# An attention block whose query and key norms move from the operands to the scores, inside the instruction that takes the row maximum

## The reference

```python
def rms_norm(x, w):
    var = jnp.mean(x * x, axis=-1, keepdims=True)
    return w * x * jax.lax.rsqrt(var + 1e-6)
def attn(h):                                  # h: 2 x 512 x 512, 32 heads of 128
    q, k, v = h @ Wq + bq, h @ Wk + bk, h @ Wv + bv
    q, k = rms_norm(q, gq), rms_norm(k, gk)   # over all 4096 columns
    a = softmax(einsum('bhqd,bhkd->bhqk', q, k) / sqrt(128))
    return einsum('bhqk,bhkd->bhqd', a, v) @ Wo + bo
x = x + layernorm(attn(layernorm(x)))
x = x + layernorm(ffn(layernorm(x)))          # a base matrix and 8 gated low-rank experts
```

## Time and profile before

| What | Value |
|---|---|
| Time, median of 3 runs | 1174.58 us (1172.68 to 1175.04) |
| Time of the profiled execution | 1176.83 us |
| Its span, first to last instruction | 1175.0 us |
| TensorE busy | 1130.2 us (96%) |
| VectorE busy | 848.8 us (72%) |
| GpSimd busy | 724.2 us (62%) |
| ScalarE busy | 663.2 us (56%) |
| Mean granted TensorE clock | 0.989 of full speed |
| Chain that ended last: TensorE / VectorE | 91% / 4% |

### The profile page before, as it was taken

The page is one execution under the profiler, slowest core; times in us unless marked ns, Lnnn a source line. Parts: engine busy times, 40 slices in busy tenths (PEclk is TensorE's granted clock), DMA queues, the critical chain, the costliest instruction groups (busy, mean ns, idle before and its releaser), DMA issues.

```text
span 1175.0 us, 17897 instructions
## 1 busy us (share of the span) xinstructions
PE 1130.2 (96%) x5704; PEld 955.7 (81%) x5704; DVE 848.8 (72%) x1304; ACT 663.2 (56%) x1331; POOL 724.2 (62%) x360
## 2 busy tenths in 40 slices
PE   6999999999999699999999999999999999999796
PEld 5788888888888588888888888888888888888575
DVE  6445545545454688888888888888888888888886
ACT  4333333333333667767767767767767767776432
POOL 2543443444437867777777777777777777774522
PEclk9999999999999899999999999999999999999899
DMA  5634434334344477887776776876776776876501
GB/s 181 216 117 151 145 123 161 134 134 161 116 152 161 125 156 162 184 154 164 184 162 153 185 161 152 184 164 152 183 163 152 183 164 152 181 149 141 143 1 71
DMA packets 302972, 178.55 MB, mean 152 GB/s; under 512 B 269536, under 2 KB 269664, under 8 KB 298720
## 3 DMA queue, kind: packets, MB, share of 16 engines
q1 hardware_dynamic: 302944, 178.19, 59.8%
HBM read 75.40 MB, written 35.65 MB: 95 GB/s over the span
## 4 chain that ended last, share of the span: by engine, by line
PE 91%; DVE 4%; DMA 2%; ACT 1%; issue 1%; SPq 1%; POOL 0%; DVEq 0%; ACTq 0%
PE ps L834 30%; PE ps L832 30%; PE ps L833 30%; DMA wa_stage<-w_qk 1%; ACT ps L678 1%; DVE neg_max L1265 1%; DVE stats L1113 1%; DVE ptl L1286 1%; DVE qk_lo L1286 0%; DMA y<-x 0%; DMA pair_k<-pair_q 0%; PE ps L842 0%; PE ps L890 0%; SPq L276 0%; DVE rms_row L1221 0%
## 5 line engine op out<-in xcount | busy, mean ns | idle before, releaser
L402 POOL TENSOR_TENSOR acc<-acc,squares 128x1024 f32<-128x1024 f32 x60 | 144.8, 2414 | 192.1 <-ACT squares L590 192.1
L448 POOL TENSOR_TENSOR qk_lo<-qk_in,qk_hi 128x1024 fp32r<-128x1024 f32 x64 | 178.5, 2790 | 125.1 <-ACT qk_hi L647 125.1
L1184 DVE TENSOR_SCALAR qk_out<-ps,tab 128x512 f32<-128x512 f32 x128 | 103.2, 808 | 165.8 <-ACT squares L590 165.7
L590 ACT ACTIVATE squares<-ps,q_k_bias 128x512 f32<-128x512 f32 x128 | 87.7, 687 | 230.1 <-PE ps L834 230.0
L678 ACT ACTIVATE ps<-ps,neg_max 128x512 f32<-128x512 f32 x256 | 168.8, 659 | 74.5 <-DVE neg_max L1265 74.5
L1265 DVE TENSOR_REDUCE neg_max<-ps 128x1 f32<-128x512 f32 x256 | 169.5, 686 | 49.6 <-PE ps L834 49.6
L834 PE MATMUL ps<-xh,wa_lo 128*128 128x512 f32 x512 | 204.5, 399 | 0.0
L832 PE MATMUL ps<-xh,wa_hi 128*128 128x512 f32 x512 | 201.6, 394 | 2.5 <-DVE xl L1168 1.5
L833 PE MATMUL ps<-xl,wa_hi 128*128 128x512 f32 x512 | 202.0, 394 | 0.0
L1279 DVE SCALAR_TENSOR_TENSOR pair_q<-ps,row_inv,pair_q 128x512 f16<-128x512 f32 x256 | 174.4, 743 | 8.4 <-ACT pair_q L687 4.5
L833 PE MATMUL ps<-wv_lo,xh 128*128 128x256 f32 (+1 forms) x544 | 157.1, 289 | 0.0
(11 more groups left out here) (132 smaller groups left out, 2400.2 us busy)
## 6 DMA issues: line engine op xcount, KB each, us to landing
q_k_scratch<-qk_out SPq DMA_DIRECT2D x32, 1024.0 KB, 4.7
qk_in<-q_k_scratch SPq DMA_DIRECT2D x64, 512.0 KB, 4.6
wa_stage<-w_qk SPq DMA_DIRECT2D x32, 512.0 KB, 5.6
wv_stage<-w_v SPq DMA_DIRECT2D x16, 512.0 KB, 5.1
wo_stage<-w_o SPq DMA_DIRECT2D x16, 512.0 KB, 5.1
y<-x SPq DMA_DIRECT2D x8, 256.0 KB, 6.0
y<-bo SPq DMA_DIRECT2D x8, 256.0 KB, 4.1
pair_k<-pair_q SPq DMA_TRANSPOSE x128, 4.6
```

What stands on the lines that cost most here:

```text
L402: pool.tensor_tensor(acc[:, w, :], acc[:, w, :], squares[:, par, w, :], ALU.add).then_inc(acc_ready, 1)
L448: pool.tensor_tensor(qk_lo[:, s % 2], qk_in[:, s], f32(qk_hi[:, s % 2]), ALU.subtract).then_inc(qk_lo_ready, 1)
L1184: dve.tensor_scalar(qk_out[:, par, w, b * S:(b + 1) * S], ps[:, 4 * par + g, :], tab[:, w, bass.ds(h, 1)], tab[:, 2 + w, bass.ds(h, 1)], A ...
```

## The change

Queries and keys are used unscaled. `scale_qk`, `rms_row` and the spreading of the queries' factors go. The queries' factors stay one number per partition (`q_factor`, times 1/sqrt(128)), and only the keys' are spread (`k_row`). `maximum` becomes a `tensor_tensor_reduce`: scores x `k_row` x `q_factor`, written back to the same bank, with the row maximum in `row_max`; after every second block VectorE waits for it and a small `tensor_scalar` makes the negative. The high half of queries and keys moves from ScalarE to GpSimd (`split_qk`), and `low_pt` moves from VectorE to GpSimd, behind `high_pt` (at the very end of stage B two casts stay on VectorE). The order of items 0 to 3 is new: item 0's scores come right after the last projection, more of the value products are placed between the first items, and batch 1's factors come later. The stage for `w_base` is now `z`, so that load waits for nothing.

```diff
@@ sync
-            sp.wait_ge(qk_scaled, 4 * PAIRS)
             sp.dma_start(wb_stage, w_base).then_inc(ffn_loaded, 16)
@@ gpsimd
+            def split_qk(p, s, m):
                 pool.wait_ge(qk_loaded[s], 16 * p + 16)
-                pool.tensor_tensor(qk_in[:, s], qk_in[:, s], rms_row[:, :, b * S:(b + 1) * S],
-                                   ALU.mult).then_inc(qk_scaled, 1)
+                if not (isinstance(m, int) and m < 2):
+                    pool.wait_ge(scores_ready, 4 * m - 4)
+                pool.sem_inc(qk_begun, 1)
+                pool.tensor_copy(qk_hi[:, s % 2], qk_in[:, s]).then_inc(qk_hi_ready, 1)
                 pool.wait_ge(qk_hi_ready, m + 1)
                 pool.tensor_tensor(qk_lo[:, s % 2], qk_in[:, s], f32(qk_hi[:, s % 2]),
                                    ALU.subtract).then_inc(qk_lo_ready, 1)
...
-            pool.wait_ge(rms_row_ready, 2)
-            scale_qk(0, 0)
+            split_qk(0, 1, 1)
...
+            def low_pt(n):
+                pool.wait_ge(low_turned, 16 * n + 16)
+                pool.sem_inc(ptl_begun, 1)
+                pool.tensor_copy(ptl[...], pair_k[:, 1]...).then_inc(ptl_ready, 1)
...
-                if prepare:
-                    scale_qk(p + s // 2, (s + 2) % 4)
-                if turned:
-                    high_pt(n - 1, None)
+                high_pt(n - 1, None)
+                low_pt(n - 1)
                 if prepare:
-                    low_qk((s + 2) % 4, n + 2)
+                    split_qk(p + s // 2, (s + 2) % 4, n + 2)
@@ scalar
-                if prepare:
-                    prepare_qk((s + 2) % 4, n + 2)
...
                 if first:
-                    spread(1, (YB, YB + 1))
+                    evacuate_v(1, 0, VB)
+                    evacuate_v(2, 2, OB)
@@ tensor
             pe.wait_ge(qk_lo_ready, 1)
+            pe.wait_ge(qk_out_ready, done + 6)
             scores(0, 0, first=True)
+            pe.wait_ge(wv_lo_ready, 2)
+            pe.wait_ge(qk_out_ready, done + 8)
+            v_item(0, 0, VB)
+            pe.wait_ge(acc_ready, 2 * HEADS + 8)
+            pe.wait_ge(var_ready, 5)
+            column_sums(1, YB)
+            v_item(0, 2, OB)
             pe.wait_ge(qk_lo_ready, 2)
             scores(1, 1)
+            pe.wait_ge(vl_ready, 1)
+            v_item(0, 4, VB)
+            pe.wait_ge(var_ready, 6)
+            v_item(0, 6, YB)
+            pe.wait_ge(rms_row_ready, 1)
+            spread(1, YB + 1)
+            pe.wait_ge(vl_ready, 2)
             attend(0, 0, 0)
@@ vector
-                dve.tensor_reduce(neg_max[:, sl, i:i + 1], ps[:, SCORE + i, :], AX.X, ALU.max,
-                                  negate=True).then_inc(max_ready, 1)
+                dve.sem_inc(max_begun, 1)
+                dve.tensor_tensor_reduce(ps[:, SCORE + i, :], ps[:, SCORE + i, :], key_factors(b),
+                                         q_factor[:, TB * b + i:TB * b + i + 1], -3.0e38, ALU.mult, ALU.max,
+                                         row_max[:, sl, i:i + 1]).then_inc(row_max_ready, 1)
+                if i % 2:
+                    dve.wait_ge(row_max_ready, 4 * n + i + 1)
+                    dve.tensor_scalar(neg_max[:, sl, i - 1:i + 1], row_max[:, sl, i - 1:i + 1], -1.0, None,
+                                      ALU.mult).then_inc(max_ready, 2)
...
                 inverses(n, sl)
-                if turned:
-                    low_pt(n - 1)
                 for i in range(TB):
-                    low_halves(n, sl, i, first)
+                    low_halves(n, sl, i)
```

More of the change, by code:

```diff
@@ L642, in evacuate_v, with spread @@
                                ACT.Copy, scale=V_DOWN).then_inc(vh_ready, 1)
[L644 to L656, removed]
-            square(*BY_BATCH[7], 8 * PAIRS)
[L658 to L664, removed]
+            def spread(b, bank):
+                act.wait_ge(rms_spread, b + 1)
+                act.activation(key_factors(b), ps[:, bank, :], ACT.Copy).then_inc(rms_row_ready, 1)
+            spread(0, YB + 1)
+            square(*BY_BATCH[7], 8 * PAIRS)
             act.wait_ge(stored[0], 16 * PAIRS)
@@ L692, in v_bias_column, with step @@
                 act.wait_ge(bias_ready, HEADS + n + 1)
-            def step(p, s, weights, first=False, output=True, value=True, prepare=True):
+            def step(p, s, weights, first=False, output=True, value=True):
                 n = 4 * p + s
@@ L739, in pair_of_heads, with second_head, first_weights @@
                 step(p, 3, wo_part(p + 1, 1 - par, 0, 8 * p))
-            step(0, 0, first_wo, first=True, output=False, value=False)
-            step(0, 1, nothing, output=False)
-            step(0, 2, nothing)
+            def second_head():
+                evacuate_v(4, 6, YB)
+                spread(1, YB + 1)
+            def first_weights():
+                act.wait_ge(wv_loaded, 32)
+                split_wv(1, 1, 0)
+                split_wv(1, 1, 2)
+                first_wo()
+            step(0, 0, first_weights, first=True, output=False, value=False)
+            step(0, 1, second_head, output=False)
+            step(0, 2, nothing, value=False)
             step(0, 3, wo_part(1, 1, 0, None))
@@ L754, in _ @@
             step(PAIRS - 1, 1, nothing)
-            step(PAIRS - 1, 2, nothing, prepare=False)
+            step(PAIRS - 1, 2, nothing)
             def ffn_weights():
@@ L807, in _ @@
             LAST = 4 * PAIRS - 1
-            step(PAIRS - 1, 3, nothing, value=False, prepare=False)
+            step(PAIRS - 1, 3, nothing, value=False)
             ffn_weights()
@@ L892, in column_sums, with spread @@
                 ins.then_inc(col_sums, 1)
-            def spread(b, banks):
-                for w in range(2):
-                    pe.wait_ge(diag_ready, 2 * b + w + 1)
-                    pe.matmul(ps[:, banks[w], :], ones[:, :], factors(b, w),
-                              start=True, stop=True).then_inc(rms_spread, 1)
+            def spread(b, bank):
+                pe.wait_ge(diag_ready, b + 1)
+                pe.matmul(ps[:, bank, :], ones[:, :], key_factors(b), start=True, stop=True).then_inc(rms_spread, 1)
             done = 8 * (PAIRS - 1)
@@ L986, in _ @@
             scores(2, 0)
-            values(0, 2, 0, 2)
+            pe.wait_ge(vl_ready, 4)
+            pe.wait_ge(rms_row_ready, 2)
             pe.wait_ge(otl_ready, 1)
@@ L1242, in split_v @@
                                          op1=ALU.subtract).then_inc(vl_ready, 1)
-            split_v(1, 0, 1)
-            mean_squares(1, 2)
-            diagonals(1)
-            split_v(2, 2, OB)
-            dve.wait_ge(y_set, 16 * NT)
             def add_y(count, tile, bank):
@@ L1292, in add_rows, with step @@
                     add_y(2 * n - 5 + k, 2 * ((s + 1) % 4) + k, YB + k).then_inc(y_added, 1)
-            def step(p, s, first=False, turned=True, output=True, value=True, rows=True):
+            def step(p, s, output=True, value=True, rows=True):
                 n = 4 * p + s
@@ L1310, in step @@
                     add_rows(p, s, n)
-            step(0, 0, first=True, turned=False, output=False, value=False, rows=False)
-            step(0, 1, output=False, rows=False)
-            step(0, 2, rows=False)
+            for i in range(TB):
+                maximum(0, 0, 0, i, i == 0)
+            mean_squares(1, YB)
+            inverses(0, 0)
+            for i in range(TB):
+                low_halves(0, 0, i, True)
+            split_v(1, 0, VB)
+            diagonals(1)
+            split_v(2, 2, OB)
+            step(0, 1, output=False, rows=False)
+            split_v(4, 6, YB)
+            dve.wait_ge(y_set, 16 * NT)
+            dve.wait_ge(rms_row_ready, 2)
+            dve.wait_ge(q_factor_ready, 2)
+            step(0, 2, value=False, rows=False)
             step(0, 3)
@@ L1410, in _ @@
             for i in range(TB):
-                maximum(N + 1, 1, i)
+                maximum(N + 1, 1, 1, i)
                 if i == 1:
```

79 lines of the change are left out of this document (35 added, 44 removed).

## The result

The kernel is slower: 1218.47 us (median of 4 runs, 1214.28 to 1221.62) against 1174.22 us, a ratio of 1.0374 with a 95% interval of 1.0342 to 1.0407. The prediction was 1186.6 us, with a range of 1166 to 1208. The direction was right and the size was not: +44 us instead of +12, and the time lies outside the range.

A forecast was written before the change was run, and what follows sets the result against it. TensorE bounds the kernel before, at 11.03 us an item; VectorE's chain would after, at 11.35. The terms -8.4 + 58 x 0.32 + 0.67 + 1.2 = +12.0 us on the median 1174.58 give 1186.6 us, range 1166 to 1208.

The forecast's parts named there:

- Is anything else late?: Check of stage B's other engines: GpSimd's load 8.4 to 9.9 us, below 11, and its casts hidden with 1.3 us left.
- VectorE becomes the bound through its own chain: Steady items: VectorE's serial chain takes 11.35 us, 0.32 us more than TensorE's 11.03; chance 0.50.
- the part from the reciprocal to the first low half: One term of VectorE's chain in a steady item: 1.22 us, against 1.61 before.
- The reduce instruction: New maximum on VectorE: pace 0.75 us, maximum arriving 0.86 us after its start, accumulator read included; first pair 1.74 us.
- Rival (1): Steady items: the reduce costs what a low half costs, VectorE stays under TensorE, 1167.4 us; chance 0.24.
- rival (3): Steady items: the reduce is dear, 0.93 us, period 11.85 us, 1216 us; chance 0.13 including periods between 11.6 and that.
- The first items: Start of stage B: the new order brings item 4's first maximum from 437.49 to 429.1 us, 8.4 us gained.
- The replay: Step-by-step timing of the first items: item 0's scores at 379 us, first maxima of later items at 408.1, 417.7 and 429.1.
- The sign that the prediction had named for a wrong start: In the changed profile, item 4's first maximum later than 433 us would show the forecast wrong.
- The casts are hidden: GpSimd's low cast ends 17.2 us after the item's first maximum, before TensorE's `attend` starts at 18.5 us.
- the second sign of being wrong: In the changed profile, TensorE waiting for `ptl` from GpSimd would show the forecast wrong.
- TensorE keeps its clock: Steady items: TensorE's waits of 0.3 us are too short to risk the lower clock; it may fall once among first items.

The follow-up runs named there:

- experiment 9: The changed kernel with the paired negations made by a negating tensor_reduce and `row_inv` made by ScalarE: 1194.86 us, ratio 1.0181.
- experiment 2: The changed kernel with each negation of two maxima made by a negating tensor_reduce instead of tensor_scalar: 1211.43 us, ratio 1.0332.
- experiment 8: The changed kernel with negations by tensor_reduce, `row_inv` on ScalarE and `evacuate_o` moved behind the second negation: 1175.79 us, ratio 1.0026.
- experiment 4: The changed kernel with the negations moved to ScalarE, one small copy ahead of each exponential: 1194.45 us, ratio 1.0175.
- experiment 1: The changed kernel with the old reduce in place of the new one and its negation, norm's factors left out of the scores: 1187.93 us, ratio 1.0132.
- experiment 5: The changed kernel with the old reduce, the norm's factors left out of the scores, and `row_inv` on ScalarE: 1165.81 us, ratio 0.9926.

## Why the prediction was wrong

**The step that failed** is in "Is anything else late?": "GpSimd's own load is ... 8.4 to 9.9 us, below 11", and with it the casts "hidden". It weighed GpSimd's time against the period and the casts against `attend`, and never asked which instruction of VectorE lies beside them. The load itself was right (147.28 us of 200 is 8.5 us in 11.5). But while a cast, copy or subtraction of GpSimd is under way, VectorE's small `tensor_scalar` instructions stand still: in the kernel after the negation up to 1.84 us and `row_inv` up to 1.67. The sum had no term for this. Both are links of VectorE's serial chain, and the change added one of them and filled GpSimd around the other. The price is the difference between the kernel after and experiment 9, which differ in nothing but those small instructions: 1218.8 - 1194.2 = 24.6 us of span (23.6 by the medians), made up of 4.3 at the start, 16.3 in the 58 periods, 2.7 in the last step and 1.3 in the tail.

It could have been read from the trace of before. VectorE, then GpSimd, in one of the first items and after stage B:

```profile
407.09 1.00 DVE L1272 TENSOR_SCALAR row_inv<-row_rec 128x4 f32<-128x4 f32 x1
408.01 3.44 DVE L1286 CAST ptl<-pair_k 128x2048 fp32r<-128x2048 f16 x1
...
406.17 1.90 POOL L505 CAST pth<-pair_k 128x2048 fp32r<-128x2048 f16 x1
408.02 2.35 POOL L448 TENSOR_TENSOR qk_lo<-qk_in,qk_hi 128x1024 fp32r<-128x1024 f32 x1
...
1100.82 5.21 DVE L1286 CAST qk_lo<-pair_k 128x2048 fp32r<-128x2048 f16 x1 [1.42 <-DMA pair_k<-pair_q]
...
1100.44 4.50 POOL L526 TENSOR_TENSOR wv_lo<-rms_row,wv_hi 128x2048 fp32r<-128x2048 f32 x1
```

The 0.17 us instruction lasts 1.00 us and ends 0.02 us after GpSimd's cast; the 1.23 us cast lasts 3.44 and 5.21 us and ends 1.1 us, about its own length, after GpSimd's subtraction: that is what to look for when work is moved to GpSimd. The Trainium skill ("SBUF — State Buffer", Who interferes with whom) states the rule: VectorE and GpSimd share one pair of SBUF ports, held by whoever starts first for its whole instruction, and a `tensor_scalar`, copy or cast on VectorE can need it while a `tensor_reduce` never does. The traces agree: under the cast of `pth` the negation took 1.84 us as a `tensor_scalar` (kernel after) and 0.15 as a `tensor_reduce` (experiment 2).

**Point by point:**

- *VectorE becomes the bound through its own chain.* Right, and shown by experiment 9: 11.48 us against 11.35 predicted, 7 us over the 58 periods. In the kernel after the terms add up to 11.52, and the 0.17 that they exceed the prediction by are in the part from the reciprocal to the first low half: 0.08 is `row_inv`, held, and 0.08 the hand-over to ScalarE, 0.11 us (713.48 to 713.59) where 0.03 was taken from a gap between two instructions of VectorE.
- *The reduce instruction.* The sum was right, the parts were not. The read of the accumulator is there (0.14 us) but lies under the next instruction: the pace is 0.67 us, not 0.75. The result comes late instead: the negation starts 0.93 us after the second reduction does. A pair to the next start costs 1.76 us, 1.74 predicted. Rival (1), that the reduction is free, and rival (3), that it is dear, are both refuted; (3) named 1216 us, near the result, for a reason that isn't there.
- *The first items.* -8.2 us without held instructions (experiment 9), -3.9 with them. The replay holds in its steps too: in experiment 9 the first maxima of items 2, 3 and 4 stand at 407.65, 418.10 and 429.30, where 408.1, 417.7 and 429.1 were predicted, although item 0's scores begin 5 us sooner than it had them (374.33, not 379). In the kernel after item 3 alone carries two: a negation of 1.61 us at 421.05 and a `row_inv` of 1.67 at 426.73. The sign that the prediction had named for a wrong start, item 4 later than 433 us, was there.
- *The casts are hidden.* Wrong in a second way too: TensorE waited for `ptl` 52 times, 20.1 us in all between 480 and 1100 us, the second sign of being wrong that the prediction had named. From the first maximum of the item at 707.32 the cast ends 17.7 us later (17.2 predicted), but `attend` is ready for it at about 17.6 and not 18.5, since the scores now begin 2.4 us ahead of the maximum (716.45 and 718.84) and not 0.9. Since TensorE wasn't the bound, what that cost isn't shown.
- *TensorE keeps its clock.* In the steady state yes (1.00 of full speed from 600 to 800 us). From 410 to 420 us it was 0.66 (0.83 before), a mix of the two levels 1.2 and 2.4 GHz, behind a busy time of 7.06 and in a stretch with 6.35 of 10 us.

**What stays open.** Why the long items cease behind item 14 and return at item 56 in the kernel after; the step of 0.08 us an item by which experiment 8 stays above 11.03; and whether the 11.5 us of the ordinary items is set by VectorE's chain (11.48 in experiment 9) or by the loop through `row_inv` (11.54 worked out): the two are too close to be told apart there, and only experiments 1 and 4, where VectorE's chain is short, show the loop by itself.

## What to carry to other kernels

When work moves to GpSimd, don't stop at comparing its load with the period: list VectorE's `tensor_scalar`, copy and cast instructions that lie on the serial chain, however small, and see whether a GpSimd instruction will now be under way beside each. A row of a few numbers that lasts ten times its usual time and ends with a GpSimd row is the sign; give such an instruction to ScalarE or write it as a reduction. And before a wait of an idle engine is taken away, ask what ran undisturbed in it.

## What the runs showed of the hardware

- A `tensor_scalar` of 2 or 4 numbers a partition (0.17 us) on VectorE is held to the end of a GpSimd cast, copy or subtraction under way: 1.84 us beside a cast of 1.89, 2.13 beside a subtraction of 2.40. A `tensor_reduce` of the same two numbers was not (0.15 us), nor was the reciprocal of four (0.18). Neither was `row_inv` beside GpSimd's 128x8 `rms` instruction of 1.65 us (0.17 us, experiments 1 and 2, once each). GpSimd is held in the same way by VectorE's cast (2.81 us instead of 2.36).
- Such holding can lock. In experiment 1 the loop of cast, `row_inv`, high halves, transfer and cast again kept a period of 11.50 us for some 30 items in a row, though TensorE needs 11.03; with `row_inv` on ScalarE it was 11.04 (experiment 5).
- The `tensor_tensor_reduce` on 128 x 512 values in PSUM takes 0.75 us at a pace of 0.67; its separate read of the accumulator (0.14 us) costs no pace, and an instruction that waits for the maximum starts 0.25 us after the read's row begins.
- GpSimd copies 128 x 1024 fp32 values to fp32r in 1.04 us and casts 128 x 2048 fp16 values to fp32r in 1.90, so per value the two are about alike.
